# An FFN, delta-rule attention and FFN block on one core: one 448-column FFN call in each attention frame, drawn from both FFNs, in place of calls of a whole slab of one FFN

## Time and profile before

| | |
|---|---|
| median of 3 runs | 1799.11 us (1799.0 to 1800.13) |
| the profiled execution: span | 1797.4 us |
| PE busy | 1663.3 us (93%) |
| DVE, ACT, POOL busy | 1264.9, 1227.6, 1268.2 us (70, 68, 71%) |
| granted TensorE clock, mean | 0.989 |
| HBM traffic | 12 GB/s over the span |

### The profile page before, as it was taken

One profiled execution on the slowest core, in us unless ns is written; L12 is line 12 of the kernel. 1 busy time (PEld: TensorE's weight loads), 2 busy tenths in 40 slices (PEclk: granted clock), 3 DMA queues, 4 the chain that ended last, 5 costly groups with the idle time before them and its releaser, 6 DMA issues.

```text
span 1797.4 us, 30372 instructions
## 1 busy us (share of the span) xinstructions
PE 1663.3 (93%) x10029; PEld 984.0 (55%) x10029; DVE 1264.9 (70%) x3082; ACT 1227.6 (68%) x2446; POOL 1268.2 (71%) x1549
## 2 busy tenths in 40 slices
PE   6989988999898998998999999989899999999999
PEld 4855444555454454544554554677554554544488
DVE  5376787787877668777777787767677777777331
ACT  4667676677667676767667686768677776766554
POOL 4474858778777677786776877777677768776653
PEclk9999999999999999999999999999899999999999
DMA  7100000000000000000000000000000000000000
GB/s 288 48 1 0 2 1 1 1 1 1 1 1 1 24 1 24 1 1 1 1 1 1 1 25 1 24 2 2 1 1 1 1 1 13 1 1 13 1 13 13
DMA packets 5274, 23.19 MB, mean 13 GB/s; under 512 B 640, under 2 KB 1664, under 8 KB 3584
## 3 DMA queue, kind: packets, MB, share of 16 engines
q1 hardware_dynamic: 5120, 21.26, 3.2%
HBM read 17.06 MB, written 4.19 MB: 12 GB/s over the span
## 4 chain that ended last, share of the span: by engine, by line
PE 54%; DVE 13%; POOL 12%; issue 11%; ACT 9%; POOLq 0%; DVEq 0%; ACTq 0%
PE ffn_bank L1141 35%; PE ffn_bank L1124 5%; PE att_bank L1162 4%; POOL hid_lo L593 4%; POOL pairs L622 3%; POOL pairs_lo L630 3%; PE state_bank L1200 2%; ACT state_parts L776 2%; DVE xn L874 2%; DVE terms L987 1%; DVE hid L887 1%; PE att_bank L1177 1%; DVE roots L865 1%; PE att_bank L1092 1%; ACT hid L725 1%
## 5 line engine op out<-in xcount | busy, mean ns | idle before, releaser
L1141 PE MATMUL ffn_bank<-hid_hi,w_sb 128*128 128x512 f16 (+1 forms) x2736 | 908.7, 348 | 23.2 <-ACT gate L712 11.2
L1141 PE MATMUL ffn_bank<-hid_lo,w_sb 128*128 128x512 f16 (+1 forms) x2736 | 908.7, 348 | 0.0
L593 POOL TENSOR_TENSOR hid_lo<-hid,hid_hi 128x512 f16<-128x512 f32 (+1 forms) x456 | 461.5, 1028 | 230.0 <-ACT hid_hi L701 229.9
L630 POOL TENSOR_TENSOR pairs_lo<-pairs,pairs_hi 128x448 f16<-128x448 f32 (+15 forms) x416 | 313.9, 759 | 144.8 <-ACT pairs_hi L790 138.9
L1141 PEld LDWEIGHTS ffn_bank<-hid_hi,w_sb 128*128 128x128 fp8e4 x2736 | 273.5, 100 | 226.3 <-issue 16.1
L622 POOL TENSOR_TENSOR pairs<-KQ 128x32 f32<-128x32 f32 (+15 forms) x496 | 332.2, 679 | 76.4 <-DVE KQ L914 74.9
L1141 PEld LDWEIGHTS ffn_bank<-hid_lo,w_sb 128*128 128x128 fp8e4 x2736 | 268.9, 98 | 207.7 <-issue 15.1
L790 ACT CAST pairs_hi<-pairs 128x448 f16<-128x448 f32 (+15 forms) x416 | 177.4, 440 | 132.9 <-POOL pairs L622 131.2
L701 ACT CAST hid_hi<-hid 128x512 f16<-128x512 f32 (+1 forms) x456 | 235.7, 554 | 34.7 <-DVE hid L887 34.2
L725 ACT ACTIVATE hid<-ffn_bank,par_sb 128x512 f32<-128x512 f32 (+1 forms) x304 | 171.7, 616 | 100.2 <-PE ffn_bank L1141 98.9
L1124 PE MATMUL ffn_bank<-xn_hi,w_sb 128*128 128x512 f16 (+1 forms) x608 | 206.6, 354 | 26.1 <-POOL xn_lo L580 8.7
(11 more groups left out here) (95 smaller groups left out, 2196.6 us busy)
## 6 DMA issues: line engine op xcount, KB each, us to landing
NK<-in_w SPq DMA_DIRECT2D x11, 1024.0 KB, 5.9
X<-in_x SPq DMA_DIRECT2D x7, 512.0 KB, 3.5
out<-X SPq DMA_DIRECT2D x7, 512.0 KB, 2.6
wqkvb_sb<-in_wqkvb SPq DMA_DIRECT2D x1, 1024.0 KB, 8.5
X<-in_x SPq DMA_DIRECT2D x2, 256.0 KB, 6.9
out<-X SPq DMA_DIRECT2D x2, 256.0 KB, 2.1
wout_sb<-in_wout SPq DMA_DIRECT2D x1, 256.0 KB, 8.7
par_sb<-in_par SPq DMA_DIRECT2D x1, 24.0 KB, 2.5
```

Source lines behind the costliest of these rows:

```text
L593: pool.tensor_tensor(hid_lo[layer % 2][:, m, call.cols], hid[:, u % HID_BUFFERS, call.cols], hid_hi[layer % 2][:, m, call.cols], ALU.subtr ...
L630: pool.tensor_tensor(pair(pairs_lo, i, dot), pair(pairs, DOT[dot], dot), pair(pairs_hi, i, dot), ALU.subtract).then_inc(pairs_ready, 1)
L1141: mm = nc.tensor.matmul(ffn_ps(call, j), weight(name, kk, 2 * pair + i), v[:, kk, cols], start=kk == 0 and part == 0, stop=kk == KT_FF - 1 ...
```

## The change

Each of the 18 frames now holds exactly one call, and a tick is a slot (`TICKS = SLOTS`). The calls of frames 0 to 15 have 448 columns, those of frames -1 and 16 have 256, and so have the two that stand alone: 20 calls in place of 19. `add_call` fills a call from both FFNs, so that one call may hold columns of up to three slabs: each such piece is a `Seg`. Calls 2 and 3 hold FFN 1 alone, calls 4 to 15 both, calls 16 and 17 FFN 2 alone. Where a step works on x itself (the layer norm's sum on POOL, its centring on DVE, the addition of the result on DVE), it is issued once for each segment; all other steps see one block of 448 columns.

All tables of ticks are new, and so are the leads and lags: key norm at tick 42 for 45, the products for split dots up to 22 ticks ahead for 9, their high and low parts up to 9 and 6 ahead for 4. The four retrievals stand at ticks 2, 22, 43 and 66 for 0, 21, 46 and 67, the four state updates at 16, 37, 58 and 83 for 15, 35, 60 and 80. The FFN's layer norm is at tick 52 in every frame, ends at 78, and its call begins at the next frame's tick 0. The loads of x wait for the load before in another place of SP's queue, and slab 1 is loaded behind the third piece of the weights instead of behind all. The buffer of DVE's products (`MIX_BUFFER`) now alternates over all its uses.

```diff
+WIDTHS = [256, 448, 448, 448, 448, 448, 448, 448, 448, 448, 448, 448, 448, 448, 448, 448, 448, 256]
...
+add_call((1, HALF))
+for _f in FRAMES:
+    _first = max(0, min((_f + 3) * HALF, SLABS * N) - DONE[1])
+    _second = max(0, min((_f - 1) * HALF, SLABS * N) - DONE[2])
+    _first = max(_first, WIDTHS[_f + 1] - _second)
+    add_call((1, _first), (2, WIDTHS[_f + 1] - _first))
+add_call((2, HALF))
...
-E_PROJ = {K_: 40, Q_: 51, V_: 48, B_: 43}
-E_NORM = 45
-E_OUT = 50
+E_PROJ = {K_: 41, Q_: 46, V_: 46, B_: 41}
+E_NORM = 42
+E_OUT = 49
...
-            for g in SLOTS_IN[f]:
-                for tick in ticks_of(f, g):
-                    for job in JOBS_IN[f]:
-                        for part in [p for p, e in job.ticks.items() if e == tick]:
-                            ln(part, job)
-                    attention(f, tick)
+            for tick in range(TICKS):
+                for job in JOBS_IN[f]:
+                    for part in [p for p, e in job.ticks.items() if e == tick]:
+                        ln(part, job)
+                attention(f, tick)
+                g = (f + 1) * SLOTS + tick
                 if g >= lag:
                     ffn(*STREAM[g - lag])
...
+                    for seg in call.segs:
+                        xs = X[:, seg.s % RING, m, seg.cols]
+                        done = nc.vector.scalar_tensor_tensor(xs, ffn_ps(call, j)[:, seg.at], w3_half[:, m:m + 1], xs, ALU.mult, ALU.add)
+                    done.then_inc(ffn_added, 1)
```

More of the change, by code:

```diff
@@ L90 @@
 UNITS = 3 * KT_FF
-Call = namedtuple("Call", "n off which s cols weight")
-Job = namedtuple("Job", "i kind part s n atts cols frame ticks")
-CALLS = []
[L98 to L103, removed]
+Call = namedtuple("Call", "n off segs width")
@@ new lines, with add_call @@
+Seg = namedtuple("Seg", "which s cols at")
+Job = namedtuple("Job", "i kind part s n atts cols frame ticks segs")
+FRAMES = range(-1, PARTS + 1)
+WIDTHS = [256, 448, 448, 448, 448, 448, 448, 448, 448, 448, 448, 448, 448, 448, 448, 448, 448, 256]
+CALLS = []
+DONE = {1: 0, 2: 0}
+def add_call(*amounts):
+    segs, at = [], 0
+    for which, n in amounts:
+        while n:
+            s, a = divmod(DONE[which], N)
+            size = min(n, N - a)
+            segs.append(Seg(which, s, slice(a, a + size), slice(at, at + size)))
+            DONE[which] += size
+            at, n = at + size, n - size
+    CALLS.append(Call(len(CALLS), len(CALLS) % 2 * 2, segs, at))
@@ L106, in call_of @@
+add_call((1, HALF))
[5 more added lines that the diff above has]
+add_call((2, HALF))
+assert DONE == {1: SLABS * N, 2: SLABS * N}
 def call_of(which, s, h):
-    return [c for c in CALLS if (c.which, c.s) == (which, s) and c.cols.start <= h * HALF < c.cols.stop][0]
-TICKS, PITCH = 88, 22
@@ L112 @@
-FRAMES = range(-1, PARTS + 1)
-FRAME_AT = [0, 92, 238, 377, 530, 665, 817, 968, 1113, 1266, 1422, 1574, 1727, 1879, 2031, 2186, 2336, 2488, 2640]
+    return [c for c in CALLS for seg in c.segs if (seg.which, seg.s) == (which, s) and seg.cols.stop >= (h + 1) * HALF][0]
+TICKS = SLOTS
 FIRST_TICK = 0
 STREAM = [(c, k) for c in CALLS[1:-1] for k in range(SLOTS)]
-SLOT_AT = [sum(c.weight for c in CALLS[1:-1][:i]) * SLOTS + c.weight * k for i, c in enumerate(CALLS[1:-1]) for k in range(SLOTS)]
-def frame_of(g):
-    return max(f for f in FRAMES if FRAME_AT[f + 1] <= SLOT_AT[g])
@@ L142 @@
[L142 to L156 removed]
+E_RETR = [2, 22, 43, 66]
+E_STATE = [16, 37, 58, 83]
@@ L193, in add_job @@
     if kind == "att":
[L194 removed]
+        s, cols = part // HALVES, slice(part % HALVES * HALF, (part % HALVES + 1) * HALF)
+        job = Job(len(JOBS), kind, part, s, None, atts, cols, frame, ticks, [Seg(1, s, cols, cols)])
     else:
[L196 removed]
+        job = Job(len(JOBS), kind, None, None, call.n, atts, slice(0, call.width), frame, ticks, call.segs)
     JOBS.append(job)
@@ L442, in ffn_ps @@
         def ffn_ps(call, j):
-            return ffn_bank[(call.off + j) % FFN_BANKS][:, 0:call.cols.stop - call.cols.start]
+            return ffn_bank[(call.off + j) % FFN_BANKS][:, 0:call.width]
         def width(dot):
@@ L592, in low @@
                 pool.wait_ge(hid_hi_ready, call.n * UNITS + (u + 1))
-                pool.tensor_tensor(hid_lo[layer % 2][:, m, call.cols], hid[:, u % HID_BUFFERS, call.cols], hid_hi[layer % 2][:, m, call.cols],
+                pool.tensor_tensor(hid_lo[layer % 2][:, m, 0:call.width], hid[:, u % HID_BUFFERS, 0:call.width], hid_hi[layer % 2][:, m, 0:call.width],
                                    ALU.subtract).then_inc(hid_lo_ready, 1)
```

99 lines of the change are left out of this document (51 added, 48 removed).

## The result

| | before | after |
|---|---|---|
| median of the runs | 1799.05 us (4 runs, 1793.96 to 1800.13) | 1702.82 us (4 runs, 1702.48 to 1703.29) |
| ratio | | 0.946, 95% interval 0.9448 to 0.9473 |
| profiled execution: span | 1797.4 us | 1701.5 us |
| PE busy, idle | 1663.3, 134.1 us | 1651.6, 49.9 us |
| DVE, ACT, POOL busy | 1264.9, 1227.6, 1268.2 us | 1258.3, 1251.0, 1279.5 us |

The change saves 5.4%.

The account below looks back on a forecast made before the run. PE was taken to set the end, busy 1663.3 of 1797.4 us, losing time to idle waits and clock. Savings of 73 us and costs of 36 gave a span of 1760.4, a median of 1762; range 1712 to 1812.

Parts of the forecast that it names:

- (a): PE's waits for key products before the `head_minus` dots: a later deadline after the key norm saves 31 us idle, 35 in all.
- (b): PE's two waits for `xn_lo`: the layer norm now ends ten slots before its call begins, saving 9 us.
- (c): Half-width calls beside full attention, with waits for the gate in frames 10 and 11: fewer such calls save 8 us.
- (d): PE's waits before state updates, 15.0 us: more slots between retrieval and update save 7 us.
- (e): PE's clock, 19.8 us lost behind long waits: with most waits gone, 14 us come back.
- (f): Gated first FFN layer beside two thirds of a solve on DVE in every frame: waits for `hid` add 10 us.
- (g): Key norm on PE waits for ACT, late with k after its projection: 1 us in each of 16 frames, adding 16.
- (h): POOL's block of six products before `hid_lo`: PE reaches slot 58 2.3 us before POOL is done, adding 3 us.
- (i): Frame 16 and the last stretch: slots shrink beside 16 `qk` dots and cover is lost, adding 5 us.
- (j): One more call, 18 more segments, 13 table loads on ACT: covered beside PE, 0; slab 1's load adds 1 us.
- second rival: Keys ready later at POOL's block, so PE waits for `hid_lo` in 15 frames: slower, 1835 us, chance 0.12.
- third rival: All frames become like frame 9, the best before at 93.8 us: 1718 us, chance 0.14.

## Why the prediction was wrong

What bounds the kernel and where the time could come from were read rightly: PE's idle time and its clock. A matmul of 448 columns takes the 0.189 us of the forecast, and the fixed price for each matmul that follows from the figures of the Trainium skill's page "TensorE: Matmul & The Clock Gate", section "Back-to-back issue gap", is not seen. By its own steps:

- (a) Waits for key products: forecast -31 us of idle. Measured, the idle time before the `head_minus` dots went from 36.9 us to 2.6 us, -34. The size is right and the mechanism was wrong. To begin with, 7.9 of the 36.9 us were waits for ACT's `O_low`, which the chain from the key norm does not explain. The later deadline came as computed (18.6 us from the norm at 728.42 to the first key dot at 747.03), but it is not what helped: with the norm back at tick 45 the waits stay away (1712.6), and with only the keys moved they stay (78.8 us). The leads take them away (71.4 to 1.6).
- (b) `xn_lo`: forecast -9, measured 8.7 to none.
- (c) Half-width calls: forecast -8. The waits of L1141 for the gate went from 11.2 to 0.5 us, -10.7. Only 4.9 of these lay in the frames with half-width calls, 10 and 11, where L1141 waited 5.2 us for other things too; the rest lay mostly beside whole calls.
- (d) State updates: forecast -7, measured 15.0 to 5.9, -9.
- (e) Clock: forecast -14, measured -16.4. The account of it was too simple: a wait as long as 2.4 us can leave the clock alone (last section).
- Waits that I had not put into the sum went too: in front of the query dots 8.5 to 0.1 us, in front of the projections 5.5 to 0.9, of the layer norms' matmuls 9.0 to 5.5. They are 17 us.

So (a) to (e) came to -79 where -73 was forecast, and the waits that I had left out to another -17. The larger miss is on the other side, in the +36 us of costs. Of the 29 us in (f), (g) and (h) under 2 came; of (i) and (j) most did, and the 4.7 us of busy time stand against the +1 for the matmuls. Smaller waits of the FFN's layers, in none of the steps, fell by another 8 us. Steps (i) and (j) are counted by stretches and the others by rows, so waits in these stretches are in both, and the list does not add up to the 96 us exactly.

- (g) The key norm: forecast +16, measured +0.2, one wait in the whole run. This is the step that failed most. I took from frame 6 of before that ACT is done with k 4.9 us after its projection. But there the layer norm's apply had released PE 0.93 us late and ACT at the same time, so ACT's state copies and gelus all stood between. In the changed kernel the apply starts at 720.37 and the projection at 723.78, 3.4 us later, so the state copies lie before the projection and only the gelus and casts beside it. ACT begins with k at 725.95, 0.4 us after its projection's end (725.5, estimated with the 1.73 us of the forecast), and is done with it at 727.5, 2.0 us after that end for the 4.9 before:

```profile
720.37 1.09 ACT L698 ACTIVATE xn<-xn,par_sb,ln_gain 128x256 f32<-128x256 f32 x2 [1.23 <-DVE xn L884]
...
725.95 0.48 ACT L750 ACTIVATE k_sq<-att_bank,par_sb 128x256 f32<-128x256 f32 x1
```

  The run with a late apply shows the wait that I had priced, 9.9 us of it, with 4.2 us more for beta, in 20 us of time. The price was that of another order.
- (f) First layer beside the solve: forecast +10, measured: `hid` 7.6 to 9.0. Frames 6 and 13, from which it came, had the retrieval at tick 0. The run with that tick in the new frames has 21.0 us of these waits, where I had written 20; two ticks later they are 9.0.
- (h) POOL's block of six products: forecast +3, and the second rival rested on it. PE's waits for `hid_lo` are 3.2 us, all of them in the first and the last frames. The first product starts 8.2 us after the key norm (728.42 to 736.60), for 7.7 before, and the order holds:

```profile
736.60 4.99 POOL L629 TENSOR_TENSOR pairs<-KQ 128x448 f32<-128x448 f32 x6 [6.42 <-DVE KQ L925]
```

- (i), (j): forecast +6. The idle time of the last stretch is 8.7 us for 5.9, +3; the first is 2.3 us longer. ACT's thirteen more table loads (159 for 146) lie beside PE, as assumed.

Why was the third rival, which came true, at 0.14? I held the like-phased frames 6 and 13 for the best witnesses of the new kernel, and the run with all old ticks shows that they were good witnesses, of that kernel: 1802 measured, 1808 forecast. What they could not tell is what ticks found for one phase would do. The rows gave no price for that, and I mended the old order wait by wait and then charged its other waits to the new one, in (f) and (g) at up to the price that frame 6 showed. The interaction is as large as the result: calls alone +1, new attention ticks in old calls +43, both with the layer norms and lags -96.

What stays open: which smallest set of the new ticks carries the gain. Taking a group out costs 10 to 229 us, and adding up to three to the old ticks never gains; the order in which they pay was not found. The four chunks' ticks were not set back as a group, and whether the lags of the engines matter was not tested.

## What to carry to other kernels

When the engines beside PE have 30% of their time free and PE still waits, the tables that set the order are one object: a wait's price read in one order does not hold in another in which its neighbours have moved by two ticks, and a group of ticks judged alone may even have the wrong sign. An order that fits one frame fits all sixteen only where the pattern repeats in phase and in width; with the phase alone, in the one case tried, two thirds of the gain stayed. A forecast for such a change should give real weight to the best frame that the old trace shows, since a fitted order can make all frames like it.

## What the runs showed of the hardware

Short waits cost no clock here: in the changed kernel the clock was granted in full in frames 0 to 14 (1.00 in each window) with idle times of about 1 us in each, in waits of at most 0.7 us.

For longer waits the length alone does not decide. In the run with all old ticks PE waits 2.5 us at the same place in each frame. Behind nine of the first fifteen such waits the clock fell, as behind the first one here, where the second matmul pair takes 0.5 us in place of 0.35; behind six it stayed full, as behind the other:

```profile
302.78 0.32 PE L1190 MATMUL att_bank<-pairs_hi,head_minus 128*128 128x352 f16 x1 [2.53 <-POOL pairs_lo L639]
...
303.47 0.52 PE L1154 MATMUL ffn_bank<-hid_hi,w_sb 128*128 128x448 f16 x1
...
503.44 0.32 PE L1190 MATMUL att_bank<-pairs_hi,head_minus 128*128 128x352 f16 x1 [2.52 <-POOL pairs_lo L639]
...
504.12 0.35 PE L1154 MATMUL ffn_bank<-hid_hi,w_sb 128*128 128x448 f16 x1
```

The windows behind the two, columns as in the earlier trace rows:

```profile
302.80:306.20 3.40, 3.22 (x11) 1.22 (x12) 3.16 (x11) 1.30 (x5) 3.40 (x5) 0.61 0.01 2
503.40:506.70 3.30, 1.99 (x11) 0.90 (x11) 3.06 (x11) 1.35 (x5) 3.30 (x5) 1.00 0.00 0
```

In the kernel before, frame 1 had 10.6 us of idle PE, in waits of up to 2.4 us, at a clock of 1.00, while frame 6 stood at 0.98 with 6.8 us of idle. With uneven widths, the same wait of 1.55 us was followed by a fall of the clock in two narrow frames of seven. These runs give no length from which on a wait costs clock.
